# Both normalisations ahead of layer 0's heads applied by ScalarE, with sums, weight remainders and a wait in another order

## What is computed

```python
x = x + L0_xattn(ctx, layernorm(x), ...)        # 16 heads of 64; context asks, x and context answer
x = x + L0_ffn(layernorm(x), ...)               # 8 experts, the best 2 of each token
x = x + L1_xattn(layernorm(x), ctx, ctx, ...)   # 16 heads of 16
x = x + L1_ffn(layernorm(x), ...)

def L0_xattn(x, latents, ln1w, ln1b, ln2w, ln2b, Wq, Wkv, Wo):
    xn, latn = ln(x) * ln1w + ln1b, ln(latents) * ln2w + ln2b
    q = latn @ Wq
    k, v = split(concat([xn, latn]) @ Wkv)
    return merge(softmax(q k^T / 8) v) @ Wo
```

## Time and profile before

| | us |
|---|---|
| median of 3 executions | 1758.63 (1755.77 to 1760.08) |
| the profiled execution | 1755.63 |
| span of its profile | 1753.9 |
| TensorE matmul busy | 1547.8 (88%) |
| VectorE busy | 1238.9 (71%) |
| GpSimd busy | 903.4 (52%) |
| ScalarE busy | 705.2 (40%) |

### The profile page before, as it was taken

How to read it: one execution, slowest core, us unless ns; L and a number is a source line. 1 busy time by engine, 2 the same in 40 slices (tenths; PEclk the granted TensorE clock), 3 DMA queues, 4 the chain that set the end, 5 groups by cost and what they waited for, 6 DMA issues and landing times.

```text
span 1753.9 us, 44902 instructions
## 1 busy us (share of the span) xinstructions
PE 1547.8 (88%) x18016; PEld 1272.2 (73%) x18016; DVE 1238.9 (71%) x2513; ACT 705.2 (40%) x1313; POOL 903.4 (52%) x864
## 2 busy tenths in 40 slices
PE   1889999999999999999999997499998975888798
PEld 0677778777777777777777775399987853566487
DVE  8757777777777577777777777544478768556765
ACT  1334444544444444444354443155544524233122
POOL 3236556655655156655665566367655646222322
PEclk9899999999999999999999998699999975655799
DMA  9125243434443043524343341977776455600101
GB/s 223 38 60 131 66 109 96 113 83 97 109 109 78 19 104 96 124 73 109 96 109 87 94 106 38 355 254 265 248 254 216 168 152 62 115 8 1 37 13 37
DMA packets 83474, 199.60 MB, mean 114 GB/s; under 512 B 17836, under 2 KB 40932, under 8 KB 82886
## 3 DMA queue, kind: packets, MB, share of 16 engines
q1 hardware_dynamic: 77350, 178.08, 38.4%
q0 software_dynamic: 3744, 10.26, 1.5%
q10 hardware_dynamic: 2176, 8.39, 1.3%
HBM read 104.47 MB, written 39.72 MB: 82 GB/s over the span
## 4 chain that ended last, share of the span: by engine, by line
PE 53%; DVE 20%; ACT 7%; POOL 6%; issue 5%; DMA 4%; ACTq 1%; DVEq 1%; SPq 0%; POOLq 0%
PE ps L1992 20%; PE ps L2091 11%; PE ps L2025 6%; PE ps L2071 6%; PE ps L2072 5%; DVE PR L1547 3%; POOL PR L917 3%; DMA latf<-wexp 3%; ACT hf L1228 2%; ACT hs_h L1230 2%; DVE hf L1669 2%; DVE mxs L1402 2%; POOL wst L933 2%; PE ps L2378 1%; DVE Y L1695 1%
## 5 line engine op out<-in xcount | busy, mean ns | idle before, releaser
L917 POOL TENSOR_TENSOR PR<-PT 128x512 f16<-128x512 f32 (+1 forms) x416 | 441.6, 1071 | 423.0 <-ACT PT L1134 422.3
L1134 ACT ACTIVATE PT<-ps 128x512 f32<-128x512 f32 (+1 forms) x576 | 323.5, 596 | 363.5 <-PE ps L2072 363.4
L2091 PE MATMUL ps<-V_h,PT 128*128 128x65 f16 (+1 forms) x2304 | 325.5, 197 | 26.5 <-DVE PR L1547 21.5
L2091 PE MATMUL ps<-V_l,PT 128*128 128x65 f16 (+1 forms) x2304 | 321.0, 195 | 0.0
L2091 PE MATMUL ps<-V_l,PR 128*128 128x65 f16 (+1 forms) x2304 | 319.6, 195 | 0.0
L2091 PE MATMUL ps<-V_h,PR 128*128 128x65 f16 (+1 forms) x2304 | 319.0, 195 | 0.0
L2091 PEld LDWEIGHTS ps<-V_h,PT 128*128 128x128 bf16 (+1 forms) x2304 | 227.0, 99 | 122.0 <-issue 49.3
L1402 DVE TENSOR_REDUCE mxs<-ps 128x1 f32<-128x736 f32 x256 | 234.8, 917 | 48.6 <-PE ps L2025 48.5
L2071 PE MATMUL ps<-QA,KA 128*128 128x512 f32 (+1 forms) x576 | 247.7, 430 | 6.0 <-DMA QB<-maxT 4.9
L2072 PE MATMUL ps<-QB,KB 65*128 65x512 f32 (+1 forms) x576 | 230.9, 401 | 0.0
L2091 PEld LDWEIGHTS ps<-V_l,PT 128*128 128x128 bf16 (+1 forms) x2304 | 229.0, 99 | 0.6
(11 more groups left out here) (352 smaller groups left out, 3626.5 us busy)
## 6 DMA issues: line engine op xcount, KB each, us to landing
wup<-wsplit SPq DMA_DIRECT2D x46, 1024.0 KB
QA<-Q_h SPq DMA_DIRECT2D x64, 256.0 KB, 4.6
latf<-wexp SPq DMA_DIRECT2D x32, 512.0 KB, 4.2
wsplit<-wst SPq DMA_DIRECT2D x32, 512.0 KB
KA<-K_h SPq DMA_DIRECT2D x32, 275.5 KB, 3.1
KA<-K_l SPq DMA_DIRECT2D x32, 275.5 KB, 4.0
KB<-K_h SPq DMA_DIRECT2D x32, 275.5 KB, 5.5
QB<-Q_l SPq DMA_DIRECT2D x32, 256.0 KB, 5.4
```

The costliest lines, as they stand in the source:

```text
L917: nc.gpsimd.tensor_tensor(PR[0:m, s % RING, :], PT[0:m, s % RING, :], upper(s)[0:m], ALU.subtract).then_inc(s_rem_pool, 1)
L1134: nc.scalar.activation(PT[0:m, s % RING, :], score_banks[s % 2][0:m], ACT.Exp, scale=HD ** -0.5).then_inc(s_exp, 1)
L2091: mm = nc.tensor.matmul(pv_bank[:, q, :], p, v, start=(kt == 0 and q == 0 and k == 0), stop=(kt == KT - 1 and k == 3), skip_group_check=True)
```

## The change

The application of both normalisations moves from VectorE to ScalarE (`once`, `twice`), with the bias -mean * rstd made by GpSimd (`latent_scales`). VectorE keeps the sums; they, the scales and the applications are set at other jobs. The first pair's projections begin one job earlier (QK0_AT 8), the bound of the value weights four jobs earlier (BOUND_AT 5), and its all-reduce ahead of GpSimd's remainder of job 10. ScalarE rounds the value weights at k = 9, VectorE makes both halves of their remainder (at k = 10 and behind the loop). The value products of batch 0 no longer wait for the remainders of batch 1; that wait stands behind them. Layer 1's waits on s_nb count from 8 on.

```diff
--- before.py
+++ after.py
@@ -43,9 +43,9 @@
 JOBS = 12
 VJOBS = 2 * KT
 MAX0_T = 2 * TB + 1
-BOUND_AT = 9
+BOUND_AT = 5
 WQK0_AT = 5
-QK0_AT = 9
+QK0_AT = 8
 AWJOBS = 6
 CASTS = 7
 E0, F0 = 8, 1024
@@ -282,6 +282,7 @@
         s_dve = sem("vector_chain")
         s_var = sem("variances_ready")
         s_rstd = sem("rstds_ready")
+        s_once = sem("latents_once_normalised")
         s_lnc = sem("context_normalised")
         s_ln = sem("latents_normalised")
         s_lat_full = sem("latent_bank_full")
@@ -847,8 +848,15 @@
             nc.gpsimd.affine_select(out=ident[:], in_=ident[:], compare_op=ALU.not_equal, fill=1.0, base=0,
                                     pattern=[[-1, P]], channel_multiplier=1).then_inc(s_const, 1)
             rstds(pool)
-            for g in (0, 1, 0, 1):
+
+            def latent_scales(g):
                 rstds(pool, 4 * g)
+                pool.wait_ge(s_rstd, powers[0])
+                cols = slice(4 * g, 4 * g + 4)
+                nc.gpsimd.tensor_tensor(ln_tmp[:, 2, cols], ln_tmp[:, 1, cols], ln_tmp[:, 4, cols], ALU.mult).then_inc(s_nb, 1)
+
+            for g in (0, 1):
+                latent_scales(g)
 
             def split(raw, parts, loaded, n, done):
                 pool.wait_ge(loaded, 16 * n + 16)
@@ -868,16 +876,18 @@
                                         lat["h"][:, b, c, cols].bitcast(F32), ALU.subtract).then_inc(s_lat_lo, 1)
 
             for k, (b, c, h) in enumerate(LATJOBS):
+                if k == 2:
+                    for g in (2, 0, 1):
+                        latent_scales(g)
                 if k == 4:
-                    rstds(pool, 8)
-                    rstds(pool, 12)
-                if k in (5, 6):
-                    rstds(pool, 4 * (k - 3))
+                    latent_scales(3)
+                    latent_scales(2)
+                if k == 8:
+                    latent_scales(3)
+                if k == 10:
+                    pool.wait_ge(s_bounds, 1)
+                    nc.gpsimd.partition_all_reduce(bound[:], bounds[:], P, RMAX).then_inc(s_bound, 1)
                 latents_lo(k, b, c, h)
-            pool.wait_ge(s_wvh, 1)
-            nc.gpsimd.tensor_tensor(wv["l"][:, 0], wv_raw[:, 0], wv["h"][:, 0].bitcast(F32), ALU.subtract).then_inc(s_wv, 1)
-            pool.wait_ge(s_bounds, 1)
-            nc.gpsimd.partition_all_reduce(bound[:], bounds[:], P, RMAX).then_inc(s_bound, 1)
             split(wo_raw, wo, s_wo_raw, 0, s_wo)
 
             def sort_constants(g):
@@ -1067,8 +1077,38 @@
                 part, cols = Q if j < 2 else K, QK_COLS[j]
                 nc.scalar.copy(part["h"][:, cols], bk[:, 0:cols.stop - cols.start]).then_inc(s_cast, 1)
 
+            def once(n, g):
+                act.wait_ge(s_nb, n)
+                for t in range(4 * g, 4 * g + 4):
+                    ins = nc.scalar.activation(Y[:, t, :], X[:, t, :], ACT.Identity, bias=ln_tmp[:, 2, t:t + 1],
+                                               scale=ln_tmp[:, 4, t:t + 1])
+                ins.then_inc(s_once, 1)
+
+            def twice(n, g):
+                act.wait_ge(s_nb, n)
+                for t in range(4 * g, 4 * g + 4):
+                    ins = nc.scalar.activation(Y[:, t, :], Y[:, t, :], ACT.Identity, bias=ln_tmp[:, 2, t:t + 1],
+                                               scale=ln_tmp[:, 4, t:t + 1])
+                ins.then_inc(s_ln, 1)
+
             act.wait_ge(s_in, 16 * 6)
             for k, (b, c, h) in enumerate(LATJOBS):
+                if k == 2:
+                    once(1, 0)
+                    once(2, 1)
+                if k == 4:
+                    once(3, 2)
+                    twice(4, 0)
+                    twice(5, 1)
+                if k == 6:
+                    once(6, 3)
+                    twice(7, 2)
+                if k == 9:
+                    act.wait_ge(s_wv_raw, 16)
+                    for i in range(NC):
+                        nc.scalar.copy(wv["h"][:, i], wv_raw[:, i]).then_inc(s_wvh, 1)
+                if k == 10:
+                    twice(8, 3)
                 act.wait_ge(s_lat_full, k + 1)
                 n = HALF if h < 2 else SP
                 w = 2 if h < 2 else 0
@@ -1080,10 +1120,6 @@
                 if k >= QK0_AT:
                     round_qk(k - QK0_AT, k - QK0_AT, first_qk_bank(k - QK0_AT))
 
-
-            act.wait_ge(s_wv_raw, 16)
-            for c in range(NC):
-                nc.scalar.copy(wv["h"][:, c], wv_raw[:, c]).then_inc(s_wvh, 1)
 
             def values(b, job):
 
@@ -1257,7 +1293,7 @@
                 round_first(j)
 
             def apply_group(n, g, part):
-                act.wait_ge(s_nb, n + 1)
+                act.wait_ge(s_nb, 2 * GR + n + 1)
                 src = X if part else Y
                 for t in range(4 * g, 4 * g + 4):
                     ins = nc.scalar.activation(Y[:, t, :], src[:, t, :], ACT.Identity, bias=ln_tmp[:, 2, t:t + 1],
@@ -1331,14 +1367,13 @@
 
             def first_sums(g):
                 dve.wait_ge(s_x[g], 16)
-                ln_sums(dve, X, 4 * g, 4)
+                ln_sums(dve, X, 4 * g, 4, negative=True)
+                lns[0] += 1
 
             def second_sums(g):
-                ln_apply(dve, X, Y, 4 * g, 4)
-                ln_sums(dve, Y, 4 * g, 4)
-
-            def second_apply(g):
-                ln_apply(dve, Y, Y, 4 * g, 4, s_ln)
+                dve.wait_ge(s_once, g + 1)
+                ln_sums(dve, Y, 4 * g, 4, negative=True)
+                lns[0] += 1
 
             def rest_qk(j, cast, bk):
 
@@ -1348,17 +1383,24 @@
                 nc.vector.tensor_tensor(part["l"][:, cols], bk[:, 0:n], part["h"][:, cols].bitcast(F32),
                                         ALU.subtract).then_inc(s_jobfree, 1)
 
-            for step in (first_sums, second_sums, second_apply):
-                for g in range(2):
-                    step(g)
+            def rest_value_weights(i):
+                dve.wait_ge(s_wvh, i + 1)
+                nc.vector.tensor_tensor(wv["l"][:, i], wv_raw[:, i], wv["h"][:, i].bitcast(F32), ALU.subtract).then_inc(s_wv, 1)
+
+            first_sums(0)
+            first_sums(1)
             for k, (b, c, h) in enumerate(LATJOBS):
+                if k == 2:
+                    first_sums(2)
+                    second_sums(0)
+                    second_sums(1)
                 if k == 4:
-                    first_sums(2)
                     first_sums(3)
-                if k in (5, 6):
-                    second_sums(k - 3)
-                if k in (7, 8):
-                    second_apply(k - 5)
+                    second_sums(2)
+                if k == 8:
+                    second_sums(3)
+                if k == 10:
+                    rest_value_weights(0)
                 dve.wait_ge(s_lat_full, k + 1)
                 dve.wait_ge(s_lat_hi, k + 1)
                 if k >= 2:
@@ -1381,8 +1423,7 @@
                                             apply_absolute_value=True).then_inc(s_bounds, 1)
                 if k >= QK0_AT:
                     rest_qk(k - QK0_AT, k - QK0_AT + 1, first_qk_bank(k - QK0_AT))
-            dve.wait_ge(s_wvh, 2)
-            nc.vector.tensor_tensor(wv["l"][:, 1], wv_raw[:, 1], wv["h"][:, 1].bitcast(F32), ALU.subtract).then_inc(s_wv, 1)
+            rest_value_weights(1)
             for j in range(len(LATJOBS) - QK0_AT, 5):
                 rest_qk(j, j + 1, first_qk_bank(j))
             dve.wait_ge(s_bound, 1)
@@ -2054,9 +2095,9 @@
 
             for j in range(len(LATJOBS) - QK0_AT, 5):
                 project_qk(j, 0, j, first_qk_bank(j))
-            pe.wait_ge(s_lat_lo, len(LATJOBS))
             pe.wait_ge(s_wv, 2)
             values(0, 5)
+            pe.wait_ge(s_lat_lo, len(LATJOBS))
 
             def scores(g, s):
                 h, half, kt = s // (2 * KT), s // KT % 2, s % KT
```

## The result

| | before | after |
|---|---|---|
| median of the first 6 executions of each, us | 1758.27 | 1744.16 (1740.58 to 1750.21) |
| profiled execution, us | 1755.63 | 1740.58 |
| its span, us | 1753.9 | 1738.8 |
| last key remainder ends | 59.87 | 49.21 |
| first score product | 99.40 | 87.75 |

The ratio is 0.9925, 95% interval 0.9908 to 0.9943: faster, by 14.1 us. I had forecast faster by 7.1, and the range (1746.5 to 1757.0) does not hold 1744.16. Two more sets of executions of the same two kernels gave 0.9948 [0.9929, 0.9968] (8.6 us between medians) and 0.9925 [0.9900, 0.9951] (13.6 us).

The account below looks back on a forecast made before the run. VectorE's list and the value weights at its end were taken to bound the prologue. The relisted schedule moved the last key remainder from 59.89 to 52.8, so 1758.6 - 7.1 = 1751.5 us; range 1746.5 to 1757.0.

Parts of the forecast that it names:

- The mark: End of the last key remainder in the prologue, 59.89 us before the change, forecast at 52.8: 7.1 us earlier.
- VectorE's list: VectorE's prologue order without the applications: sums, context jobs and second sums, with second sums of group 2 ending at 26.6.
- ScalarE's: Eight groups of four normalisation activations in ScalarE's prologue, priced from layer 1 at 2.08 us each, 2.02 counting overlap.
- The bias: One added GpSimd multiplication per group in the prologue; scale 1.06, both 1.66 us by layer 1's row.
- from 44.05, at the low clock: TensorE's last prologue burst: transposes and projections 2 to 4 at the low clock, ending at 51.8.
- rival B: Last projection burst at full clock: mark 49.8, gain 10 us, 12 with some value products also at it; chance 0.18.
- Everything behind it shifts whole: All behind the first score product (99.40 us) stays as before, so the time falls by as much as that product moves.
- case A: The forecast itself: 7.1 us gained in the prologue, 5.5 to 8.6 with small errors; chance 0.54.
- The last weight remainder: VectorE's second half of the value weights' remainder, 51.0 to 52.3, taken at 1.3 us, 3.04 at the high price.
- Rival D: VectorE's small operations on sums slow beside GpSimd; two groups eat the gain, four make it 1765; chance 0.07.
- Rival C: ScalarE's groups (2.4 instead of 2.0) or last weight remainder (3.04) cost more: 1754.7; chance 0.21.
- The moved wait: Batch 1's remainders, ending near 60, awaited behind the value products; in front, over 5 us would be lost.

Follow-up runs that it names:

- first and third profile: Profiles of the unedited changed kernel from its first and third sets: medians 1744.16 and 1744.65 us, each 0.9925 of the kernel before.
- the nine with this order of projections: Profiles of the changed kernel (three) and of its edits: wait in front, one application twice, weights rounded earlier (twice), filling matmuls, and both together; medians 1742.09 to 1750.81 us.
- its second profile: The kernel before, unedited, profiled again: median 1755.79 us, ratio 0.9992; first score product at 97.42 instead of 99.40.
- the second profile: The changed kernel, unedited, profiled again: median 1745.81 us, ratio 0.9948 to the kernel before; first score product at 90.52.
- the run with the old tail: Only the normalisations moved to ScalarE, with the prologue's end (bound, value weights, first projection, wait) as in the kernel before: 1746.19 us, ratio 0.9951.
- all fourteen profiles: All profiles taken: the kernel before (two), the changed kernel (three) and the edited runs; medians 1742.09 to 1758.27 us.

## Why the prediction missed

- **The mark** was rightly chosen: all that was won lies ahead of the score product, and the order of events came as listed, TensorE's wait ahead of job 10 among them (3.57 us, released by group 3's second application).
- **VectorE's list** came out as forecast (second sums of group 2 end at 26.5; 26.6 forecast); **ScalarE's** groups took the 2.08 us of the row they were priced by, one after the other.
- **The bias was mis-sized**: 0.52 forecast, 0.20 measured. The first projection started at 34.75 instead of 35.5, and group 3's application ended at 43.3 instead of 44.0: 0.7 us of the miss. The bias is 0.3 of that, since one hand-over of it lies on the chain (second applications of group 1 from 22.7 instead of 23.0); the rest is small errors in ScalarE's list, whose next group started at 26.5 instead of 27.2. The row of layer 1 that gave 0.52 had VectorE beside it, at five operations with two inputs in SBUF:

```profile
1455.40 2.84 DVE L1695 SCALAR_TENSOR_TENSOR Y<-og,rw,Y 128x256 f32<-128x256 f32 x5
```

I had looked at the neighbour for the price of the weights' remainder and not for this one; that it made the bias longer is likely, not tested.
- **The step that failed** is "from 44.05, at the low clock". I priced transposes and three projections at 1.2 GHz throughout, 7.7 us to the end of projection 4. In the first and third profile they ran at 2.4 GHz and took 4.2 us (43.37 to 47.5), in the second partly so. That is 3.6 us less, of which 0.7 was lost again, because VectorE's last weight remainder and the key remainders around it now end 1.7 us behind projection 4 instead of 1.0: 2.9 us of the mark's 3.6. My reason against the full clock was the gap, by the window at 60 to 61 of the kernel before; there the low clock came behind a gap of 3.58 us, and here the full clock stayed through one of 3.57. My rival B was this case, with its last key at 49.8 (measured 49.2) and 12 us with some of the value products (measured 11.65 at the score), and I gave it 0.18; two of three profiles of the unedited kernel were it, and four of the nine with this order of projections.
- **The sum of the miss**, 7.0 us: 3.6 at the mark, 1.0 in the value products, which had the full clock sooner (they too are open to chance: the kernel before gained 2.0 there in its second profile), and some 2.4 behind the score product.
- **"Everything behind it shifts whole"** holds in the mean, but not in one pair: 3.45 us of the difference between the first two profiles lie behind the score product, within its scatter. In the set of the second profile the medians differ by 8.6 us, which is the upper end of my case A, in the other two by 14.1 and 13.6: how far I was off also hangs on the set. I had put the scatter of a median into C's end of the range and not into B's; that is why the range missed by 2.3 us.
- **The last weight remainder** took 1.21 us (forecast 1.3, no GpSimd reader beside it); the first took 1.92 beside a lat_l, hidden as said. In the run with the old tail it was 2.82 beside GpSimd's own. The Trainium skill, "SBUF — State Buffer", section "Who interferes with whom", says that a VectorE instruction with two inputs in SBUF contends with a GpSimd instruction that reads SBUF. All three agree: 1.21 us alone, and in the other two it ended 1.1 us behind the end of GpSimd's instruction (44.21 behind 43.12, and 50.68 behind 49.60).
- **Rival D** did not come: VectorE's small operations kept at 0.16 us, but for one of 0.53 at 34.19, where GpSimd was at lat_l 7. **Rival C** did not come. The moved wait was needed as reckoned, with the late remainders ending at 60.06 (forecast near 60).

## What to carry to other kernels

Work taken off the engine that heads the chain is worth what the new head of the chain allows: walk each engine's list in order with durations from rows, and do it for each level that the clock can take: here a burst behind a gap of 2.65 to 3.61 us on TensorE ran at either, in one and the same kernel. Look what a neighbour was doing in the row from which a price is taken. When a kernel's single executions scatter by 10 us, put that scatter at both ends of the range, and split a measured difference at the last event that the edit can touch before explaining it. Here the rearranged end of the prologue was worth nothing while VectorE headed the chain (last key 2.0 us later), and at most 2.4 us at the last key once it no longer did.

## What the runs showed of the hardware

Between the same two instructions, with no edit, the granted clock was 1.00 in one execution and 0.50 in another: in the changed kernel's burst at 44 us (full behind gaps of 3.57 and 3.61 us, low behind one of 2.65), and in the value products of the kernel before (at 64 us: 1.00 in one profile, 0.50 in the other). A two-input operation on GpSimd with 4 columns took 0.20 us in the changed prologue, and 0.52 in the row of layer 1 by which I had priced it, beside VectorE's two-input operations. Around the all-reduce GpSimd's list stood still, with no wait in the profile that explains it: 6.9 us before its own 0.37 and 7.1 after it in the first changed profile, 6.19 and 7.54 in the kernel before, and 5.5 to 7.4 and 6.8 to 7.5 over all fourteen profiles, wherever it was put.
